# A fused attention and mixture-of-experts layer: one shared pair moved from the front to the end, the 80th routed tile dropped, the last weights' splits moved, the last routed second product issued one step earlier

## The reference, cut to what matters

```python
x = layernorm(x + attention(x))          # x: 2 x 1024 x 256, 16 heads, 4 key/value heads, causal
scores = sigmoid(x @ gate_w.T) + gate_b  # 16 experts
weights, indices = top_k(scores, 4)      # weights normalised to a sum of 1
shared = silu(x @ w1_s) * (x @ w3_s) @ w2_s          # every token
routed = sum over its 4 experts of weight * (silu((x @ w1_e) * (x @ w3_e)) @ w2_e)
x = layernorm(x + shared + routed)       # hidden width of an expert: 176
```

## Time and profile before

| | us |
|---|---|
| median of 3 runs | 566.12 (565.82 to 566.49) |
| the profiled execution's own time | 566.13 |
| its span, first to last instruction | 564.4 |
| PE busy | 529.9 (94%) |
| DVE busy | 439.0 (78%) |
| ACT busy | 369.7 (65%) |
| POOL busy | 295.4 (52%) |
| PE's clock, share of full speed | 0.985 |

### The profile page before, as it was taken

How to read it: one execution, slowest core, us unless ns; L and a number is a source line. 1 busy time by engine, 2 the same in 40 slices (tenths; PEclk the granted TensorE clock), 3 DMA queues, 4 the chain that set the end, 5 groups by cost and what they waited for, 6 DMA issues and landing times.

```text
span 564.4 us, 12218 instructions
## 1 busy us (share of the span) xinstructions
PE 529.9 (94%) x3801; PEld 360.5 (64%) x3801; DVE 439.0 (78%) x1122; ACT 369.7 (65%) x831; POOL 295.4 (52%) x341
## 2 busy tenths in 40 slices
PE   8999999999999899989999898899999999999880
PEld 4646444445454354535433487799999999999760
DVE  2387989899889799999992269987787878785682
ACT  2444767787887598868688574467676767676132
POOL 5121231655313657358978773777544444545671
PEclk9999999999999899989999999999999999999996
DMA  5954174400632912321132541576444334320892
GB/s 145 172 72 58 30 194 132 83 4 20 99 82 64 210 37 60 64 78 60 41 124 76 164 139 40 166 247 209 153 134 134 112 117 127 117 88 6 315 355 74
DMA packets 53741, 64.95 MB, mean 115 GB/s; under 512 B 8123, under 2 KB 47438, under 8 KB 53680
## 3 DMA queue, kind: packets, MB, share of 16 engines
q1 hardware_dynamic: 45952, 46.45, 32.1%
q0 software_dynamic: 7104, 17.60, 8.9%
q10 hardware_dynamic: 624, 0.13, 0.1%
HBM read 32.49 MB, written 25.76 MB: 103 GB/s over the span
## 4 chain that ended last, share of the span: by engine, by line
PE 71%; DVE 13%; POOL 6%; issue 4%; ACT 2%; DMA 2%; SPq 1%; ACTq 0%; POOLq 0%; DVEq 0%
PE psH L1670 14%; PE psS L1475 10%; PE psO L1460 9%; PE psT L1445 8%; PE psS L1537 4%; POOL xs_scratch L753 3%; DVE MX L1139 3%; PE psG L1681 3%; PE psX L1638 3%; PE psS L1480 2%; PE psY L1693 2%; PE psY L1697 2%; PE psY L1694 2%; PE psY L1695 2%; PE psY L1696 2%
## 5 line engine op out<-in xcount | busy, mean ns | idle before, releaser
L878 ACT ACTIVATE prob<-psT 128x512 f32<-128x512 f32 (+3 forms) x384 | 167.4, 495 | 54.9 <-PE psT L1445 52.3
L1139 DVE TENSOR_REDUCE MX<-psS 128x1 f32<-128x512 f32 (+3 forms) x344 | 183.1, 595 | 11.8 <-PE psS L1480 6.0
L1475 PE MATMUL psS<-KS,QS 96*128 96x512 bf16 (+3 forms) x384 | 110.9, 330 | 4.9 <-DVE MX L1139 2.5
L824 POOL DMA_INDIRECT y_scratch<-ys,dst x80 | 77.9, 973 | 68.9 <-ACT ys L1033 54.0
L1445 PE MATMUL psT<-QS,KS 98*128 98x512 bf16 (+3 forms) x384 | 107.7, 330 | 1.8 <-DMA QS<-MT 0.9
L782 POOL TENSOR_SCALAR_AFFINE_SELECT prob<-prob 128x512 f32<-128x512 f32 x64 | 42.3, 663 | 98.1 <-ACT prob L878 97.9
L1460 PE MATMUL psO<-prob,V 128*32 128x512 f32 (+3 forms) x768 | 82.7, 505 | 1.1 <-POOL prob L782 1.0
L1670 PE MATMUL psH<-wU,xh 128*128 (+1 forms) x384 | 81.7, 334 | 0.1
L753 POOL DMA_INDIRECT xs_scratch<-x1row,slotu x64 | 65.7, 1026 | 26.9 <-issue 16.2
L1445 PEld LDWEIGHTS psT<-QS,KS 98*128 98x128 bf16 x384 | 33.9, 98 | 54.8 <-ACT prob L878 35.4
L1475 PEld LDWEIGHTS psS<-KS,QS 96*128 96x128 bf16 x384 | 37.4, 99 | 46.1 <-DVE MX L1139 23.7
(11 more groups left out here) (252 smaller groups left out, 1005.8 us busy)
## 6 DMA issues: line engine op xcount, KB each, us to landing
xs<-xs_scratch SPq DMA_DIRECT2D x80, 134.0 KB
y<-y_scratch SPq DMA_DIRECT2D x16, 512.0 KB, 10.8
QS<-qp SPq DMA_DIRECT2D x48, 128.0 KB, 5.1
wU_raw<-in_L_ffn_w_routed_dram SPq DMA_DIRECT2D x32, 176.0 KB, 3.6
xs_scratch<-padrow SPq DMA_DIRECT2D x1, 2144.0 KB
xs_scratch<-padrow SPq DMA_DIRECT2D x16, 134.0 KB
x1row<-in_L_attn_x_dram SPq DMA_DIRECT2D x4, 512.0 KB, 6.8
out_dram<-x1row SPq DMA_DIRECT2D x8, 256.0 KB, 2.8
```

What stands on the lines that cost most here:

```text
L824: nc.gpsimd.indirect_dma_start(y4_dram, bass.IndirectOffsetOnAxis(ap=dst[:, n % NSEL, t:t + 1], axis=0), ys[:, n % NYS, t, :], None, bound ...
L878: nc.scalar.activation(prob[:, step % NPROB, h, 0:HALF - c0], ps[:, 0:HALF - c0], ACT.Exp).then_inc(s_Tfree, 1)
L1139: nc.vector.tensor_reduce(out=MX[:, c0 // HALF, heads[0]:heads[-1] + 1, i - TH * q], in_=src, op=ALU.max, axis=AX_X).then_inc(s_Sfree, 1)
L1475: last = mm(ps[:, e * dist:e * dist + cols], QS[0:ROWS, QAT[(k // 2) % NSLOT], g % 2 * G + h, (i - TH * q) * P:(i - TH * q + 1) * P], KS[b ...
```

## The change

Five edits. `EARLY` becomes 3: routed pairs are m = 3 to 42, and five shared pairs follow. The weights of the last seven units are split earlier: ACT rounds two units at i = -2 and two at i = -1, one at i = 0, and the last two ahead of the late items of i = 1; POOL makes the low parts of the first five, the first of them already after the first layer-norm power, and DVE makes those of the last two, with a semaphore of their own. The last routed pair has one tile: PE's loops go over `tiles_of(m)`, POOL sends 79 tiles, SP waits for 79. `down(LASTR)` is issued ahead of `up` in its step instead of behind the transposes, and ACT's `scaled(LASTR)` ahead of its copy of `h1`. ACT still scales both halves of that pair's `psY`.

```diff
-EARLY = 4
+EARLY = 3
+MOST = (B * T * TOPK - P) // P + NE
+assert MOST == NTILE - 1
...
-LAST_AT = {-2: LASTU[0:1], -1: LASTU[1:3], 0: LASTU[3:UNDER], 1: LASTU[UNDER:]}
-LOWS_AFTER = {1: LASTU[0:1], 2: LASTU[1:2], 3: LASTU[2:]}
+LAST_AT = {-2: LASTU[0:2], -1: LASTU[2:4], 0: LASTU[4:UNDER]}
+LOWS_AFTER = {0: LASTU[0:1], 1: LASTU[1:2], 2: LASTU[2:3], 3: LASTU[3:UNDER]}
...
# SP
-                sp.wait_ge(s_ysc[i], 32 * ((NRP - i + NYS - 1) // NYS))
+                sp.wait_ge(s_ysc[i], 16 * len([n for n in range(MOST) if n // 2 % NYS == i]))
# POOL, send(n)
+                    if 2 * n + t == MOST:
+                        return
# ACT
+            def last_split(u):
+                act.wait_ge(s_w[u], 32)
+                hi, lo, raw = weight_part(u)
+                nc.scalar.copy(hi, raw).then_inc(s_whi2, 1)
...
                     split_rows(i + 2)
+                if i - 1 == LASTR:
+                    scaled(LASTR)
                 if 0 <= i + 1 < NPAIR:
                     first_hidden(i + 1)
+                if i + 1 == EARLY - 1:
+                    for u in LASTU[UNDER:]:
+                        last_split(u)
...
-                if i - 1 == LASTR:
-                    scaled(LASTR)
# DVE
                 if 0 <= i + 1 < NPAIR:
                     product(i + 1)
+                if i + 1 == EARLY - 1:
+                    for u in LASTU[UNDER:]:
+                        dve.wait_ge(s_whi2, LASTU.index(u) + 1)
+                        hi, lo, raw = weight_part(u)
+                        nc.vector.tensor_tensor(lo, raw, hi.bitcast(F32), ALU.subtract).then_inc(s_wlo3, 1)
# PE
+            def tiles_of(m):
+                return range(1 if m == LASTR else 2)
...
-                for t in range(2):
+                for t in tiles_of(m):        # in rows_back, up, gated_back and down
...
                 if m == EARLY:
-                    pe.wait_ge(s_wlo2, len(LASTU))
+                    pe.wait_ge(s_wlo2, UNDER)
+                    pe.wait_ge(s_wlo3, len(LASTU) - UNDER)
...
                     pe.wait_ge(s_y0, m)
-                    pe.wait_ge(s_y1, m)
+                    if m != LASTR:
+                        pe.wait_ge(s_y1, m)
...
                     rows_back(i + 2)
+                if i - 1 == LASTR:
+                    down(LASTR)
                 if 0 <= i + 1 < NPAIR:
                     up(i + 1)
...
-                if i - 1 >= 0:
+                if i - 1 >= 0 and i - 1 != LASTR:
                     down(i - 1)
```

More of the change, by code:

```diff
@@ L455, in attention_moe @@
         s_wlo2 = sem("s_wlo2")
+        s_wlo3 = sem("s_wlo3")
         s_wlob = sem("s_wlob")
@@ L1051, in _ @@
                     run(item)
-                if i - 1 == LASTR:
-                    scaled(LASTR)
                 for u in LAST_AT.get(i, ()):
-                    act.wait_ge(s_w[u], 32)
-                    hi, lo, raw = weight_part(u)
-                    nc.scalar.copy(hi, raw).then_inc(s_whi2, 1)
+                    last_split(u)
             for n in range(NSHP):
@@ L1665, in up @@
                     pe.wait_ge(s_z, m)
-                for t in range(2):
+                for t in tiles_of(m):
                     e = expert(m, t)
```

## The result

| | before | changed |
|---|---|---|
| median, us (20 runs each) | 566.55 (564.58 to 574.19) | 571.78 (569.07 to 577.99) |
| profiled execution, us | 566.13 | 569.93 |
| its span | 564.4 | 568.2 |
| PE / DVE / ACT / POOL busy | 529.9 / 439.0 / 369.7 / 295.4 | 528.6 / 438.1 / 369.3 / 290.5 |
| mean granted clock of PE | 0.985 | 0.978 |

The changed kernel is slower: ratio 1.0079, 95% interval 1.0054 to 1.0104. The forecast was 566.6 us, half a microsecond slower than before, with a range of 564.6 to 568.4. The sign came out as forecast, the size didn't: 0.8% and not 0.1%, outside the range.

The account below looks back on a forecast made before the run. It took DVE to bound the step from attention to routed pairs and PE the routed pairs, so PE's end of `down(47)` counts; -2.0 + 1.15 + 0.35 + 0.95 = +0.45 on 566.12 gave 566.6 us, range 564.6 to 568.4.

Parts of the forecast that it names:

- The 80th tile: Term for the last routed pair: one tile less takes half a pair's matmuls off PE, -2.0 us.
- The front: Term for one shared pair less before the routed pairs: without the sends, R7 would come at -0.7 us.
- R7: Start of PE's step i = 7, 366.48 us before; forecast to move by +1.15 us with the sends counted.
- (d): Front step: `up(3)` waits for DVE's low parts, 0 to 1.0 us on PE, mostly hidden; 0.1 taken for DVE.
- The sends: ACT's third `ys` waits for send(0), landing 2.7 us after issue; R7 moves +1.15 us, paid once.
- the rule that R7, in effect, is at least the landing less 1.05: Step 7 cannot start earlier than send(0)'s landing minus 0.20 and 0.85 us of permitted ACT lag: 367.63.
- Rival 3: Send(0) lands late, its queues shared with loads, padding writes and scatters; at 4.5 us, 568.4 us; chance 0.15.
- `down(42)` ahead of `up`: Term for the moved product near the end: PE idles waiting for ACT's scaling to free `psY`, +0.35 us.
- The adds into the last pair: Term at the end: POOL's earlier adds delay DVE's `w_` of pair 47, and PE with it, +0.95 us.
- what would show it: Trace signs: ACT waiting 1.5 to 2.5 us before its third `ys`; pair 47's `w_` longer than 0.52 and 0.25.
- Rival 1: The last pair escapes POOL's adds, by phase or a later first load: 565.6 us; chance 0.18.

Follow-up runs that it names:

- f4: Kernel before with only the unused 80th tile taken out (four shared pairs first, old splits, `down(42)` in its old place): 565.93 us, ratio 1.0017.
- g2: Kernel before without the 80th tile, POOL's adds held until the last pair's `w_` is written: 564.29 us, ratio 0.9984.
- h4: Repeat of g2, kernel before without the 80th tile and with POOL's adds held: 564.84 us, ratio 1.0003.
- g1: Changed kernel with nine idle products of 512 columns on PE ahead of `up(3)`: 574.67 us, ratio 1.0154.
- i2: Changed kernel with three `ys` buffers, eight `sel` slots, `down(42)` back behind `up`, POOL's adds held, and nine idle products: 564.20 us, ratio 0.9967.
- f3: Changed kernel with `down(42)` and its scaling put back in their old places: 570.48 us, ratio 1.0111.
- f1: The changed kernel itself run again as a control, on another chip: 570.75 us, ratio 1.0102 to the kernel before.
- i1: Changed kernel with three `ys` buffers, eight `sel` slots, `down(42)` back behind `up`, POOL's adds held, no idle products: 565.34 us, ratio 0.9997.
- h3: Changed kernel with SP's padding-row writes issued later, four at a time behind loads 12 to 15: 574.53 us, ratio 1.0193.
- g3: Changed kernel with `EARLY = 4`, four shared pairs first and four last: 568.49 us, ratio 1.0023.
- g4: Changed kernel with nine idle products, a third `ys` buffer, `down(42)` back behind `up`, and POOL's adds held: 567.49 us, ratio 1.0029.
- f2: Changed kernel with a third `ys` buffer: 570.83 us, ratio 1.0107.

## Why the prediction was wrong

- **The 80th tile, -2.0:** right. Steps 41 to 45 take 14.0 instead of 16.0 us in f4, g2 and h4.
- **The front, R7 before the sends at -0.7:** wrong, it came 1.5 later than before. The failed step is (d), "Bound: 0 to 1.0 us on PE, mostly hidden by DVE; I take 0.1 for DVE". The parts were right: two low parts in 1.7 us (predicted 1.8), no blocked `w_`. But the gate's copy stood behind them on DVE, so PE waited 1.84 us, and I had counted such a wait only as time. It cost both. The clock is the larger part, 1.45 us on `up(3)` (with idle products, g1 and i2, the front is 46.4). The rest is 0.7 us that remain at full clock: steps 1 to 3 take 18.1 us in g1 and 17.4 before. The gain of 0.7 that was forecast did come, in steps 4 to 6 (14.5 instead of 15.2 us), and is used up by it. That this rest is the stop is likely, but no run took the stop away.
- **The sends.** That ACT's third `ys` would wait for send(0), 1.5 to 2.5 us, was right (2.53), and the rule that R7, in effect, is at least the landing less 1.05 was 0.5 too strict (369.4 by it; step 8 less 4.0 is 368.9). Wrong was the size of the landing (2.7 taken, 3.0 to 6.2 measured; the upper bound of 4.8 came from one send of one execution). The earlier trace rows was read rightly as bytes: in that trace POOL's queue had moved 1.36 MB from 354 to 368.6 us, as much as eight scatters and send(0). But bytes moved are not yet landed. The same count is reached at 370.0 in the changed kernel, at 369.1 in g1 and at 368.5 in i2, and ACT went on 0.5, 2.6 and 3.1 us after that, if the queue works in order. Wrong above all was the step "The sends follow one another at 4.0 us or less, so it is paid once". They are issued some 3.9 us apart, but each lands after another delay (3.0, 3.8, then 5.15 us), and ACT waited three times. The term was +1.85 over the front alone; it is 3.8, of which step 7, the one that was forecast to pay, has 1.46. Rival 3, a late landing with a price of 568.4 at 4.5 us, is the nearest, and it had 0.15; but it spoke of send(0) alone and was to decide from 3.4 us on, and in this execution send(0) landed after 3.0. No rival had the wait come back. The Trainium skill's page "DMA: Bandwidth & Descriptors" (Anatomy of one DMA) gives 2.3 us for one tile, an estimate by its fit; that is farther off than my row, and I had only let it argue downward.
- **`down(42)` ahead of `up`, +0.35:** 1.2 measured (f3: 3.41 + 4.03 against 3.99 + 4.64). PE's wait for `ys` was 0.32, as worked out. Missed was what the order takes away: `down(42)` used to stand between `up(44)` and `up(45)` and covered ACT's copy and DVE's `z` of pair 44. Without it PE waits again, 0.39 at 518.97, behind `psX` and `psG` that had run out already.
- **The adds into the last pair, +0.95:** the mechanism was right, the price depends on the execution. By "what would show it" the forecast was to be wrong if the two `w_` were at their usual length, and in this execution they were. The adds begin 6.5 us ahead of `w_` of pair 47 (predicted 6.4). In two of three executions of the changed kernel they leave it alone, because `w_` falls into a pause in which POOL waits for a load (0.92 us at 531.23); in one they cost 2.9, clock included. In f4 they cost 1.4. Rival 1 named this phase. The Trainium skill's page "SBUF — State Buffer" (SBUF: two separate sides) states an exclusive lock of the shared ports, and the traces agree with it: `w_` goes from 0.77 to between 1.3 and 2.4 us in all beside the adds, and back to 0.77 when they are held (g2). The long end of f1 may be one reason why the medians differ by 5.2 us where the profiled executions differ by 3.8; no run counts how often it comes.
- **The account closes.** From before's span of 564.4: start -0.6, front +1.5, sends +3.8, tile -2.0, move +1.2, and -0.1 elsewhere: 568.2. i1 takes out sends, move and port and should be 564.0 to 564.4; it is 563.9. That agreement is partly luck: i1 started 0.7 us earlier than the kernel before, and its sends cost 1.0 us and not 0.1 to 0.4. The account is one of stages, each from single profiled executions. The kernels of i1, i2, g2 and h4, in which most costs are gone, are not told from the kernel before by their times.

What stays open: why the landings are so long and so different. It isn't the padding rows alone (h3). It isn't how busy the DMA engines are either: from 364 to 371 us their share is 0.84 in the changed kernel, 0.82 in g1 and 0.84 in i2, and send(0) landed after 3.0, 5.6 and 6.2 us. I did not try fewer scatters ahead of the sends, nor three shared pairs first with the splits in their old places. Nor do I know when a stop of PE costs its clock: below.

## What to carry to other kernels

A wait on an engine that seems covered is to be priced twice, as time and as clock: look up what a stop of that length did to the granted clock elsewhere in the trace. Taking a step of slack from a ring of buffers is paid as often as the transfers are late, not once; bound the landing by the longest of many transfers, and look for every ring that the same landing releases (`ys` and `sel` here). When a ring's size is changed, check that the semaphore index of each wait still names the transfer that is meant. When an instruction is moved, ask what it covered in the old place, and where work that ends earlier will now meet a neighbour's port.

## What of the hardware was not expected

- PE's clock fell to 0.50 behind stops of 1.84 us (changed), 1.94 (g3), 1.59 (f1) and 3.80 us (g1), and was 0.50 to 0.55 behind 1.55 us in g4, where nine products of 512 columns took 3.79 instead of 2.11 us. It stayed at 1.00 behind 1.23 us before the first ranks, but also behind 2.20 (f2), 2.30 (f4) and 2.34 us (g3) ahead of the last gated transposes. So the stop's length alone doesn't decide.
- An indirect scatter of one tile lands 3.0 to 6.2 us after its issue in this stretch, in the same kernel differently each time, and at nearly the same DMA share (0.82 to 0.84).
- The same code reached step -2 at 317.7 to 320.2 us in different executions; a difference of 2 us in a single profiled span is no result. Only the stages can be compared at this size.
- One chip gave 600 us for a kernel that the others run in 566. Its four traces have standstills of ACT of 8.3 to 11.9 and of some 5 us, and step -2 came at 327.0 to 329.9 us, so the attention part too was 7 us or more longer. The cause is not known.
